# Cross-attention and the experts' shared part put into one block: the last two tiles' norm, logits and rank stand between the first pieces of the shared expert

## The chip, the cores and the metric

One NeuronCore of one Trainium2 chip. The metric is device time in microseconds (us) of the whole program, one launch, fp32 in and out; lower is better. The kernel before takes 1863.8 us (median of 3 runs).

## What is computed

One decoder layer without a norm at its end, on 4096 tokens (64 sequences of 64) of width 256:

```python
x = x + attn(layernorm(x))                     # 32 heads of 64, 8 KV heads, RoPE, causal, sinks
x = x + xattn(layernorm(x), ctx, ctx)          # 8 heads; softmax over (256 x 256) per head
h = layernorm(x)
logits = h @ router_w.T                        # 8 experts, top 1, score = sigmoid(top logit)
routed = sum_e down_e(up_e(xr_e) * silu(gate_e(xr_e)))    # xr_e = score * h for the expert's tokens
shared = (silu(h @ gate_w) * (h @ up_w)) @ down_w         # 256 -> 512 -> 256, for all tokens
x = x + shared + routed
```

## The kernel before, in words

Three blocks stand one after the other; between two blocks all engines wait for each other. Each engine (TensorE PE, ScalarE ACT, VectorE DVE, GpSimd POOL, and SyncE SP, which issues most DMAs) has a stream of its own, written out by hand; semaphores join them. Nothing reorders a stream: an instruction that waits holds up all behind it on its engine.

- `attention`: 32 tiles of 128 tokens. It leaves the stacked operands of the second attention in DRAM.
- `cross`: 32 tiles. A tile t goes through five stages, each in the body of a later tile: scores and row maxima (t), turned scores and exponentials (t+1), the sums over the values (t+2, `nd`), division by the denominators and the residual `x2` (t+3), then norm, transposed norm `xn3T`, logits, argmax, rank within the expert, and the scatter of the scaled row into its expert's list (t+4). The denominators go through DRAM: `nd` to `xden` by DMA, reciprocal on DVE (`invert`), out to `inv_d` and back, broadcast, as `xrden` (`inverses_out`, `inverses_in`), then `quotient` on POOL. So after tile 31's scores four more bodies follow (t = 32 to 35), the last two of which (t = 34 and 35) hold only the division, norm and routing of tiles 30 and 31. POOL also splits the shared expert's weights here into a high and a low part (`wshh`, `wshl`).
- `experts`: first the shared expert in 64 pieces n (16 groups g of 256 tokens, 4 columns of the 512 wide hidden layer each). PE does in piece n `up_s(n, 0)` (gate) and `up_s(n, 1)` (up), 6 matmuls of 256 columns each, then `down_s(n-1)`, 6 more. Between them stand ACT `gate_s` (Silu) and `high_h` (copy), DVE `hidden_s` and `low_h`. Per group, SP loads `xs` (`load_x`, 256 KB from `xn3T_d`) and the residual `xb` (`load_base`), and stores `base_d` (`store`); ACT `high_x` and POOL `low_x` split `xs`. Meanwhile DVE makes the table of the routed tiles (`count_tiles` to `pad_rows`), SP sends it through DRAM (`tab_d`, `tabr`), POOL writes 8 padding scatters, and ACT issues the loads of the experts' weights, 1.5 MB each, at pieces 2, 6, ... 30. Then the routed tiles: 40 of 128 rows, through `wexp`.

In `experts` SP's order for group g, and PE's for the pieces, are:

```python
for g in range(1, NG + 1):
    if 2 <= g + 1 < NG:
        load_x(g + 1)
    store(g - 1)
    if 2 <= g + 1 < NG:
        load_base(g + 1)
    if g == 4:  # tab_d out, wait for it, tabr in
```

Of the kernel before, what the change touches and what calls it, by code (L numbers as in the profile page):

```python
# [8 lines left out]
F32 = mybir.dt.float32  # L9
# [773 lines left out]
def cross(nc, A, G, NT, NRT):  # L783
# [6 lines left out]
    with ExitStack() as pb:  # L790
# [3 lines left out]
        def bank(name, n=1):  # L794
            return pb.enter_context(nc.psum_tensor(name, [P, n, 512], F32))

        bS = bank("bankX", 4)
        bT = bank("bankXT", 2)
        bN = bank("bankN")
        bM = bank("bankM")  # L800

# [9 lines left out]
        wraw = sb("wraw", [P, WE])  # L811
# [35 lines left out]
        G.s_scat = s_scat  # L847
# [8 lines left out]
            sem(n) for n in ("s_f3p", "s_f3", "s_lg", "s_top", "s_esc", "s_oh1", "s_rank", "s_pos", "g_sc", "c_fin", "s_xr3"))  # L856

# [19 lines left out]
        def tiles(eng, body):  # L877
# [12 lines left out]
        block = pb.enter_context(nc.Block())  # L890

        @block.sync
        def _(sp):
# [25 lines left out]

            def body(tile, one, two, three, four, five):  # L920
# [13 lines left out]
                if five:  # L934
                    yp = y[1] % 2
                    sp.wait_ge(s_x2, at(y) + 1)
                    sp.dma_start(G.x2_d[bass.ds(at(y) * P, P), :], x2[yp][:]).then_inc(s_fst[yp], 16)
# [16 lines left out]
                if five:  # L954
                    if not three:
                        sp.wait_ge(s_f3, at(y) + 1)
                    sp.dma_start(G.xn3T_d[:, :, bass.ds(at(y) * P, P)].rearrange("k p n -> p k n"), xn3T[:]).then_inc(s_fst[y[1] % 2], 16)
# [5 lines left out]
            tiles(sp, body)  # L963
            for p in range(2):
                sp.wait_ge(s_fst[p], 32 * (NT // 2))

        @block.gpsimd
        def _(pool):
# [96 lines left out]
            tiles(pool, body)  # L1065

        @block.scalar
        def _(act):
# [20 lines left out]

            def scale_row(y):  # L1090
# [14 lines left out]
            def body(tile, one, two, three, four, five):  # L1105
                w, v, z, y = prev(tile, 1), prev(tile, 2), prev(tile, 3), prev(tile, 4)
                for r in range(STEPS):
# [4 lines left out]
                    if five and r == 3:  # L1112
                        act.wait_ge(s_f3p, at(y) + 1)
                        o = prev(y, 1)
                        need(act, s_fst[o[1] % 2], (pair(o) + 1) * 32)
                        nc.scalar.activation(xn3T[:], bM[:, 0, 0:D].rearrange("p (k n) -> p k n", k=2),
                                             ACT.Copy).then_inc(s_f3, 1)
                    if five and r == 5:
                        act.wait_ge(s_top, at(y) + 1)
                        nc.scalar.activation(score[:, 0:1], top8[:, 0:1], ACT.Exp, scale=-1.0).then_inc(c_fin, 1)  # L1120
# [11 lines left out]
            tiles(act, body)  # L1132

        @block.vector
        def _(dve):
# [81 lines left out]
            tiles(dve, body)  # L1217

        @block.tensor
        def _(pe):  # L1220
# [108 lines left out]
            tiles(pe, body)  # L1329


def experts(nc, A, G, NT, NRT):
# [8 lines left out]
    with ExitStack() as pc:  # L1341
# [6 lines left out]
        def bank(name, n=1):  # L1348
            return pc.enter_context(nc.psum_tensor(name, [P, n, 512], F32))

        bk = [bank(f"bankG{i}") for i in range(2)]
        bS = bank("bankU", 2)
        b4 = bank("bankH")
        bX = bank("bankY", 2)
        b7 = bank("bankI")

        wexp = sb("wexp", [P, E * WE])
        cnt, ntile, cum, ones8, ge, lim, v0, bad, ptmp2 = (
            sb(n, [P, E]) for n in ("cnt", "ntile", "cum", "ones8", "ge", "lim", "v0", "bad", "ptmp2"))
        above = sb("above", [P, E, NT])  # L1360
        ei, si, dist = (sb(n, [P, 1]) for n in ("ei", "si", "dist"))
        tabf = sb("tabf", [P, 2])
        tabi = sb("tabi", [P, 2], I32)
        padx = [sb(f"padx{e}", [P, 1], I32) for e in range(E)]
        tabr = sb("tabr", [1, 2 * P], I32)
        xin = [sb(f"xin{p}", [P, D + 1]) for p in range(2)]
        xs = [sb(f"xs{p}", [P, 2, 2 * P]) for p in range(2)]
        xsl = [sb(f"xsl{p}", [P, 2, 2 * P], F32R) for p in range(2)]
        xsh = [sb(f"xsh{p}", [P, 2, 2 * P], F32R) for p in range(2)]
        hs = [sb(f"hs{p}", [P, 2 * P]) for p in range(2)]  # L1370
        hsl = [sb(f"hsl{p}", [P, 2 * P], F32R) for p in range(2)]
        hsh = [sb(f"hsh{p}", [P, 2 * P], F32R) for p in range(2)]
        xb = [sb(f"xb{p}", [P, 2, D]) for p in range(2)]
# [10 lines left out]
        s_xin, s_yst, s_x2in, s_gat, s_out = (  # L1384
            [sem(f"{n}{p}") for p in range(2)] for n in ("s_xin", "s_yst", "s_x2in", "s_gat", "s_scout"))
        s_xsh = sem("s_xsh")
        XIN = 16 * (NG // 2)
        s_tx, s_xT, s_g, s_u, s_silu, s_h, s_th, s_hT, s_d, s_y, s_tok = (
            sem(n) for n in ("s_tx", "s_xT", "s_g", "s_u", "s_silu", "s_h", "s_th", "s_hT", "s_d", "s_y", "s_tok"))
# [11 lines left out]
        block = pc.enter_context(nc.Block())  # L1401

        @block.sync
        def _(sp):
            def load_x(g):
                need(sp, s_xT, g - 1)
                sp.dma_start(xs[g % 2][:], G.xn3T_d[:, :, g * 2 * P:(g + 1) * 2 * P].rearrange(
                    "k p n -> p k n")).then_inc(s_xin[g % 2], 16)

            def load_base(g):  # L1410
                need(sp, s_yst[g % 2], 16 * (g // 2))
                sp.dma_start(xb[g % 2][:], x2_d[g * 2 * P:(g + 1) * 2 * P, :].rearrange(
                    "(i p) d -> p i d", i=2)).then_inc(s_x2in[g % 2], 16)

            def store(g):
                sp.wait_ge(s_y, 2 * (g + 1))
                sp.dma_start(base_d[g * 2 * P:(g + 1) * 2 * P, :].rearrange("(i p) d -> p i d", i=2),
                             xb[g % 2][:]).then_inc(s_yst[g % 2], 16)
# [10 lines left out]
            for g in range(2):  # L1429
                load_x(g)  # L1430
            for g in range(2):
                load_base(g)
            for g in range(1, NG + 1):
                if 2 <= g + 1 < NG:
                    load_x(g + 1)
# [3 lines left out]
                if g == 4:  # L1439
# [17 lines left out]
        def _(pool):  # L1457
            nc.gpsimd.memset(ones8[:], 1.0).then_inc(s_ones, 1)
            def low_x(g):
                pool.wait_ge(s_xsh, g + 1)  # L1460
                nc.gpsimd.tensor_tensor(xsl[g % 2][:], xs[g % 2][:], xsh[g % 2][:].bitcast(F32),
                                        ALU.subtract).then_inc(s_xT, 1)

            for g in range(5):
                low_x(g)
# [6 lines left out]
            for g in range(5, NG):  # L1472
                low_x(g)
# [43 lines left out]
        def _(act):  # L1517
            def high_x(g):
                act.wait_ge(s_xin[g % 2], 16 * (g // 2 + 1))
                need(act, s_u, NF * (g - 1))  # L1520
                nc.scalar.activation(xsh[g % 2][:], xs[g % 2][:], ACT.Copy).then_inc(s_xsh, 1)

            def gate_s(n):
                act.wait_ge(s_g, n + 1)
                need(act, s_d, n - 1)
                nc.scalar.activation(hs[n % 2][:], bk[n % 2][:, 0, 0:2 * P], ACT.Silu).then_inc(s_silu, 1)

            def high_h(n):
                act.wait_ge(s_h, n + 1)
                nc.scalar.activation(hsh[n % 2][:], hs[n % 2][:], ACT.Copy).then_inc(s_th, 1)  # L1530
# [14 lines left out]
            high_x(0)  # L1545
            high_x(1)
            for n in range(NS):
# [4 lines left out]
                if n % NF == 2 and n // NF < E:  # L1552
                    nc.scalar.dma_start(wexp[:, n // NF * WE:(n // NF + 1) * WE], A["wexp"][n // NF]).then_inc(s_w, 16)
# [3 lines left out]
        def _(dve):  # L1557
            ch = Chain(dve, c_tab, 17, 0)

            def count_tiles():  # L1560
                dve.wait_ge(s_ones, 1)
                ch(nc.vector.tensor_tensor(cnt[:], run[:], C["base"], ALU.subtract))
# [57 lines left out]
            def hidden_s(n):  # L1620
                dve.wait_ge(s_silu, n + 1)
                dve.wait_ge(s_u, n + 1)
                nc.vector.tensor_tensor(hs[n % 2][:], bS[:, n % 2, 0:2 * P], hs[n % 2][:], ALU.mult).then_inc(s_h, 1)

            def low_h(n):
                dve.wait_ge(s_th, n + 1)
                nc.vector.tensor_tensor(hsl[n % 2][:], hs[n % 2][:], hsh[n % 2][:].bitcast(F32),
# [16 lines left out]

            for n in range(NS):
                hidden_s(n)
                low_h(n)
                if n == 1:
                    count_tiles()
                if n == 2:  # L1650
                    sum_tiles()
                if n == 3:
                    expert_of()
                if n == 5:
                    row_of()
                if n == 6:
                    tile_table()
                if n == 7:
                    pad_limits()
                if n in (9, 10):  # L1660
                    pad_rows(n - 9)
# [7 lines left out]
        def _(pe):  # L1669
            pe.wait_ge(G.s_wshh, 6)  # L1670

# [84 lines left out]
            for n in range(NS):  # L1756
                up_s(n, 0, bk[n % 2][:, 0, 0:2 * P], s_g)
                up_s(n, 1, bS[:, n % 2, 0:2 * P], s_u)
                if n >= 1:
                    down_s(n - 1)  # L1760
            turn_in((0, 0))
# [47 lines left out]

def decoder(nc, A, NT, NRT):  # L1810
    assert NT * P == NTOK and NT % 4 == 0 and NT >= 24 and NRT % 2 == 0 and NRT + NT < P
    with ExitStack() as top:
        G = Shared(nc, top, NT, NRT)
        attention(nc, A, G, NT, NRT)
        with nc.sbuf_tensor("wshh", [P, WE], F32R) as wshh, nc.sbuf_tensor("wshl", [P, WE], F32R) as wshl:
            G.wshh, G.wshl = wshh, wshl
# [53 lines left out]
```

## Time and profile before

| | us |
|---|---|
| median of 3 runs (lowest, highest) | 1863.8 (1858.2, 1870.18) |
| profiled execution: time | 1864.66 |
| its span, first to last instruction | 1862.5 |
| PE busy | 1728.7 (93%) |
| DVE busy | 1185.5 (64%) |
| POOL busy | 840.6 (45%) |
| ACT busy | 813.0 (44%) |
| mean granted clock of PE | 0.974 |

Busy times are of one profiled execution. In the row of tenths, PE stands at 9 in nearly all of 40 slices of 46.6 us; the exceptions are the first, slice 31 (5), slices 32 to 34 (7), one 7 in the attention's end, and slices 35 and 38.

### The profile page before, as it was taken

Reading aid. Unit: us, or ns where it says so; the run is one execution under the profiler, and the core shown is the slowest. Engines: PE = TensorE matmul, PEld = TensorE weight load, DVE = VectorE, ACT = ScalarE, POOL = GpSimd, SP = SyncE. Lnnn points to the kernel's source line nnn. Section 1 sums busy time; section 2 is a strip of 40 time slices with the busy share of each in tenths; the row PEclk is TensorE's granted clock in tenths of the full one; section 3 lists DMA queues with packets and bytes.
Section 4 is the critical chain, followed back from the end, with each engine's and each line's share of the span. In section 5 each row is a group of like instructions: output and inputs, shape, how many; then the busy total and the mean of one; then the engine's idle time right before and its main releaser. Section 6 shows DMA issues by size and latency. Waiting matters only on the chain. (4 is left out here: it accounts for less than half of the span.)

```text
span 1862.5 us, 45291 instructions
## 1 busy us (share of the span) xinstructions
PE 1728.7 (93%) x15345; PEld 1390.9 (75%) x15441; DVE 1185.5 (64%) x2269; ACT 813.0 (44%) x1575; POOL 840.6 (45%) x1302
## 2 busy tenths in 40 slices
PE   3999999999999999999699999999995779999997
PEld 2888888888888888888577777777773779866664
DVE  5777777777777777777478888888882334422221
ACT  3334434433433444343247777777774324311111
POOL 4554655555555465555334444444444121144443
PEclk9999999999999999999879999999998799999999
DMA  5021111111112112111234444444442453222221
GB/s 183 19 58 44 42 56 54 36 51 56 42 42 56 47 37 56 56 39 42 75 101 111 123 119 117 115 118 124 123 109 63 167 207 125 74 64 67 66 64 39
DMA packets 145343, 148.43 MB, mean 80 GB/s; under 512 B 26194, under 2 KB 139926, under 8 KB 143482
## 3 DMA queue, kind: packets, MB, share of 16 engines
q1 hardware_dynamic: 138362, 120.87, 23.6%
q0 software_dynamic: 5760, 14.06, 2.4%
q10 hardware_dynamic: 1152, 12.58, 1.9%
q8 instruction: 43, 0.70, 0.2%
q14 instruction: 26, 0.21, 0.0%
HBM read 93.46 MB, written 54.11 MB: 79 GB/s over the span
## 5 line engine op out<-in xcount | busy, mean ns | idle before, releaser
L1149 DVE TENSOR_REDUCE xmax<-bankX 128x4 f32<-128x1024 f32 x256 | 309.2, 1218 | 63.4 <-PE bankX L1234 58.1
L1102 ACT ACTIVATE xe<-bankXT 128x512 f32<-128x512 f32 x512 | 292.1, 598 | 91.2 <-PE bankXT L1245 74.9
L1245 PE MATMUL bankXT<-stq,stk 98*128 98x256 f32 x1024 | 229.4, 310 | 11.4 <-ACT xe L1102 4.9
L369 POOL TENSOR_TENSOR roped<-ropeC,ropeD 128x512 f32<-128x512 f32 x160 | 205.4, 1290 | 56.4 <-DVE ropeD L530 56.3
L1245 PEld LDWEIGHTS bankXT<-stq,stk 98*128 98x128 f32 x1024 | 155.9, 191 | 54.1 <-ACT xe L1102 31.8
L557 DVE TENSOR_TENSOR oTl<-bankV,oTh 128x512 fp32r<-128x512 f32 x128 | 88.1, 688 | 166.7 <-ACT oTh L445 166.7
L662 PE MATMUL bankQ<-wqh,xnTh 128*128 128x512 f32 x384 | 188.9, 492 | 0.0
L1234 PE MATMUL bankX<-stk,stq 96*128 96x256 f32 x1024 | 172.6, 293 | 14.2 <-DMA rw<-in_rw 10.9
L361 POOL TENSOR_TENSOR prob<-prob,rden 128x1024 f32<-128x1024 f32 x64 | 122.0, 1906 | 88.6 <-DVE rden L553 88.6
L1234 PEld LDWEIGHTS bankX<-stk,stq 96*128 96x128 f32 x1024 | 146.2, 198 | 18.2 <-DMA rw<-in_rw 11.1
L728 PE MATMUL bankO<-woh,oTh 128*128 128x256 f32 x512 | 152.5, 298 | 0.0
L662 PE MATMUL bankQ<-wql,xnTh 128*128 128x512 f32 x384 | 152.2, 396 | 0.0
L662 PE MATMUL bankQ<-wqh,xnTl 128*128 128x512 f32 x384 | 151.9, 396 | 0.0
L713 PE MATMUL bankV<-probT,vbd 128*128 128x256 f32 x512 | 136.8, 390 | 9.8 <-ACT probT L439 9.8
L728 PE MATMUL bankO<-woh,oTl 128*128 128x256 f32 x512 | 143.3, 280 | 0.0
L728 PE MATMUL bankO<-wol,oTh 128*128 128x256 f32 x512 | 143.3, 280 | 0.0
L527 DVE TENSOR_TENSOR ropeC<-bankQ,const 128x512 f32<-128x512 f32 x160 | 109.5, 684 | 40.3 <-PE bankQ L662 40.3
L1260 PE MATMUL bankN<-xe,cT 128*32 128x256 f32 x2048 | 123.8, 382 | 0.4 <-ACT xe L1102 0.4
L439 ACT ACTIVATE probT<-bankP 128x512 f32<-128x512 f32 x128 | 76.2, 596 | 108.8 <-PE bankP L639 108.8
L445 ACT ACTIVATE oTh<-bankV 128x512 fp32r<-128x512 f32 x128 | 76.7, 599 | 103.5 <-PE bankV L713 103.5
L1007 POOL TENSOR_TENSOR xpart<-nd,xrden 128x512 f32<-128x512 f32 x32 | 41.1, 1286 | 173.3 <-DMA xrden<-inv_d 173.3
L329 POOL TENSOR_TENSOR spare_g<-half_neg 128x1 f32<-128x1 f32 x130 | 25.3, 195 | 203.9 <-DVE mv L499 199.3
(196 smaller groups left out, 4022.3 us busy)
## 6 DMA issues: line engine op xcount, KB each, us to landing
stackk_d<-chl SPq DMA_DIRECT2D x96, 128.0 KB, 2.3
stackq_d<-q2hl SPq DMA_DIRECT2D x96, 128.0 KB, 2.3
stk<-stackk_d SPq DMA_DIRECT2D x32, 384.0 KB
stq<-stackq_d SPq DMA_DIRECT2D x128, 96.0 KB
wexp<-in_wexp ACTq DMA_DIRECT2D x8, 1536.0 KB
x_d<-x SPq DMA_DIRECT2D x64, 128.0 KB, 1.9
xrden<-inv_d SPq DMA_DIRECT2D x64, 128.0 KB, 2.5
xin<-xg_d SPq DMA_DIRECT2D x40, 128.5 KB, 2.1
```

The lines of the kernel that those rows point to most:

```text
L361: nc.gpsimd.tensor_tensor(v, v, rden[:, r, :].unsqueeze(2).to_broadcast([P, 16, HD]), ALU.mult).then_inc(s_pn, 1)
L369: nc.gpsimd.tensor_tensor(roped[c % 3][:], ropeC[c % 2][:], ropeD[c % 2][:], ALU.add).then_inc(s_rsum, 1)
L527: nc.vector.tensor_tensor(ropeC[c % 2][:].rearrange("p (h d) -> p h d", d=HD), src.rearrange("p (h d) -> p h d", d=HD), cos.unsqueeze(1).t ...
L557: nc.vector.tensor_tensor(oTl[g % 2][:], bV[:, 0, :].rearrange("p (a b) -> p a b", a=4), oTh[g % 2][:].bitcast(F32), ALU.subtract).then_in ...
L662: ins = nc.tensor.matmul(out, a[p][:, k, :], w[:, k, col:col + 512], start=False, stop=(k == 1 and n == 2))
L713: ins = nc.tensor.matmul(out[:, :, b, :], vbd[u[1]][b][:, g, :], src[:, :, b, :], start=True, stop=True)
L728: ins = nc.tensor.matmul(out, a[g % 2][:, j, :], w[:, 4 * g + j, :], start=False, stop=(g == 3 and j == 3 and n == 2))
L1102: nc.scalar.activation(xe[q][:].rearrange("p n m -> p (n m)"), bT[:, q % 2, :], ACT.Exp).then_inc(s_xe, 1)
L1149: nc.vector.tensor_reduce(xmax[tile[1] % 2][:, :, a:b + 1:b - a].rearrange("p m h -> p h m"), bS[:, 2 * (pr % 2):2 * (pr % 2) + 2, :].rear ...
L1234: ins = nc.tensor.matmul(bS[:, q % 4, m * D:(m + 1) * D], stq[p][0:96, hd, m * P:(m + 1) * P], stk[p][0:96, hd // 4, :], start=True, stop= ...
L1245: ins = nc.tensor.matmul(bT[:, q % 2, n * D:(n + 1) * D], stk[p][0:98, hd // 4, n * P:(n + 1) * P], stq[p][0:98, hd, :], start=True, stop= ...
L1260: ins = nc.tensor.matmul(bN[32 * j:32 * j + 32, 0, (m % 2) * D:(m % 2 + 1) * D], c[:, k, 160 * j + 32 * m:160 * j + 32 * m + 32], xe[4 * b ...
```

## The change

`cross` and `experts` share one block, so that no engine waits for the others between them. The SBUF and PSUM that both use are now allocated together (`shared_memory`); `xs`, `xb` and `hs` lie in the buffer of the shared expert's raw weights, which is free once they are split. The bodies t = 34 and 35 of `cross` are gone; what they did for tiles 30 (`prior`) and 31 (`last`) is called between the first pieces of the shared expert, on each engine at a place of its own. The loads of `xs` for groups 0 and 1 are issued before the body t = 32, their split before t = 33. The experts' weights, whose buffer overlaps those of `cross`, are loaded at pieces 18, 23, ... 53. The table is made 12 pieces later and its DMA stands at g = 6; `load_x` runs two groups ahead in SP's order.

```diff
 # cross, tiles(): the last bodies
-            for t in range(LAST, NT + 4):
+            for t in range(LAST, NT + 2):
+                ahead_of(t)
                 peeled(t)
 # SP in cross
+            def ahead_of(t):
+                if t == NT:
+                    sp.wait_ge(G.s_wshh, 6)
+                    for g in range(2):
+                        load_x(g)
 # POOL, ACT in cross
+                if t == NT + 1:
+                    low_x(0)
+                if t == NT + 1:
+                    high_x(0)
 # SP in experts
-            for g in range(2):
-                load_x(g)
             for g in range(2):
                 load_base(g)
+            load_x(2)
+            inverses_out(last)
+            inverses_in(last)
+            store_x2(prior)
+            store_xn(prior)
             for g in range(1, NG + 1):
-                if 2 <= g + 1 < NG:
-                    load_x(g + 1)
+                if g + 2 < NG:
+                    load_x(g + 2)
                 store(g - 1)
                 if 2 <= g + 1 < NG:
                     load_base(g + 1)
-                if g == 4:
+                if g == 1:
+                    store_x2(last)
+                if g == 2:
+                    store_xn(last)
+                if g == 6:
                     sp.wait_ge(s_tabi, 1)
 # POOL in experts
+            low_x(1)
             nc.gpsimd.memset(ones8[:], 1.0).then_inc(s_ones, 1)
-            for g in range(5):
+            quotient(last)
+            weigh(prior)
+            low_x(2)
+            spread(last)
+            send(prior)
+            low_x(3)
+            weigh(last)
+            send(last)
+            for g in range(4, 8):
                 low_x(g)
             pool.wait_ge(s_pad, 1)
 # ACT in experts
-            high_x(0)
             high_x(1)
             for n in range(NS):
                 gate_s(n)
                 high_h(n)
                 if n % NF == 0 and 2 <= n // NF + 1 < NG:
                     high_x(n // NF + 1)
-                if n % NF == 2 and n // NF < E:
-                    nc.scalar.dma_start(wexp[...], A["wexp"][n // NF]).then_inc(s_w, 16)
+                if n == 2:
+                    evac_norm(prior)
+                if n == 4:
+                    exp_score(prior)
+                if n == 6:
+                    scale_row(prior)
+                # 9, 11, 13: the same for last
+                if n == 18:
+                    for q in range(2):
+                        act.wait_ge(G.s_scat[q], 16 * (NT // 2))
+                        act.wait_ge(G.s_fst[q], 32 * (NT // 2))
+                if n >= 18 and (n - 18) % 5 == 0 and (n - 18) // 5 < E:
+                    e = (n - 18) // 5
+                    nc.scalar.dma_start(wexp[:, e * WE:(e + 1) * WE], A["wexp"][e]).then_inc(s_w, 16)
 # DVE in experts, after hidden_s(n) and low_h(n)
+                # 0: invert(last); 1: normalise(prior); 3: choose(prior); 5: place(prior), stats_of(last)
+                # 7: normalise(last); 10: choose(last); 12: place(last)
-                # count_tiles to pad_rows at 1, 2, 3, 5, 6, 7, 9, 10
+                # count_tiles to pad_rows at 13, 14, 15, 17, 18, 19, 21, 22
 # PE in experts, after up_s(n, 0), up_s(n, 1), down_s(n - 1)
+                # 2: turn_norm(prior); 3: logits(prior); 4: rank(prior)
+                # 9: turn_norm(last); 10: logits(last); 11: rank(last)
```

(The comment lines for DVE, PE and the second tile of ACT stand for the same `if n == k:` form as the lines shown.)

## Rows read from the trace of the kernel before

**Rows 1.** Windows: us, busy us (instructions) by engine, granted clock, DMA share, GB/s.

```profile
1410.00:1420.00 10.00, 8.64 (x84) 5.53 (x88) 2.88 (x10) 6.96 (x16) 3.08 (x4) 1.00 0.29 83
1420.00:1430.00 10.00, 2.87 (x22) 1.86 (x14) 3.18 (x16) 1.69 (x4) 4.27 (x8) 0.75 0.21 62
```

**Rows 2.** Timeline, tile 31's chain and the seam: start, duration, engine, work, idle before.

```profile
1420.79 0.37 PE L1291 MATMUL bankM<-onehot,onesf 128*128 128x8 f32 x2
...
1422.85 0.51 ACT L1095 ACTIVATE xr<-xn,score 128x256 f32<-128x256 f32 x1 [1.57 <-POOL score L1030]
...
1423.79 0.35 DVE L1158 RECIPROCAL xiden<-xden 128x32 f32<-128x32 f32 x1 [1.02 <-DMA xden<-nd]
...
1430.56 1.26 POOL L1007 TENSOR_TENSOR xpart<-nd,xrden 128x512 f32<-128x512 f32 x1 [4.26 <-DMA xrden<-inv_d]
...
1444.33 1.11 POOL L1036 DMA_INDIRECT xg_d<-xr,posx  x1 [2.16 <-DVE posx L1197]
...
1448.98 0.91 SPq L1407 DMA_DIRECT2D xs<-xn3T_d  x2
...
1453.30 1.28 ACT L1526 ACT_TABLE_LOAD   x1
...
1454.04 0.55 PE L1688 MATMUL bankG<-xsh,wshh 128*128 128x256 f32 x1 [11.27 <-POOL xsl L1461]
...
1455.70 0.38 ACT L1526 ACTIVATE hs<-bankG 128x256 f32<-128x256 f32 x1 [1.11 <-PE bankG L1688]
...
1459.23 0.28 PE L1701 MATMUL bankY<-wshh,hsh 128*128 128x256 f32 x1
```

**Rows 3.** Timeline, one tile's norm, logits and rank on PE at full clock.

```profile
1416.33 0.38 PE L1224 MATMUL bankM<-const,xn 128*128 128x128 f32 x2
...
1417.77 0.55 PE L1285 MATMUL bankM<-rw,xn3T 128*128 128x8 f32 x4
```

**Rows 4.** Timeline, undisturbed pieces of the shared expert: ACT's group period, end.

```profile
1547.77 0.62 ACT L1521 ACTIVATE xsh<-xs 128x512 fp32r<-128x512 f32 x1
1556.41 0.62 ACT L1521 ACTIVATE xsh<-xs 128x512 fp32r<-128x512 f32 x1
...
1614.40 0.38 PE L1711 MATMUL bankI<-const,xin 128*128 128x128 f32 x2
```

**Rows 5.** Waits of PE, from 1454 us: us in total, times, longest.

```profile
PE bankY L1701 <- DVE hsl L1627: 15.0, 6, 6.6
```

**Rows 6.** Timeline, the four longest waits of PE, and the Silu before the last.

```profile
1481.47 0.38 PE L1701 MATMUL bankY<-wshh,hsh 128*128 128x256 f32 x1 [2.65 <-DVE hsl L1627]
...
1500.67 0.39 PE L1701 MATMUL bankY<-wshh,hsh 128*128 128x256 f32 x1 [2.34 <-DVE hsl L1627]
...
1519.67 0.58 PE L1701 MATMUL bankY<-wshh,hsh 128*128 128x256 f32 x1 [6.64 <-DVE hsl L1627]
...
1539.03 0.37 ACT L1526 ACTIVATE hs<-bankG 128x256 f32<-128x256 f32 x1
...
1540.82 0.40 PE L1701 MATMUL bankY<-wshh,hsh 128*128 128x256 f32 x1 [1.73 <-DVE hsl L1627]
```

**Rows 7.** Waits of ACT for loads of xs, from 1454 us.

```profile
ACT xsh L1521 <- DMA xs<-xn3T_d: 14.0, 3, 7.6
```

**Rows 8.** Timeline of SP's queue around the table at g = 4.

```profile
1505.44 0.47 SPq L1441 DMA_DIRECT2D tab_d<-tabi  x1
1513.76 0.26 SPq L1443 DMA_DIRECT2D tabr<-tab_d  x1
1514.07 0.39 SPq L1407 DMA_DIRECT2D xs<-xn3T_d  x1
```

**Rows 9.** Windows in the shared expert, columns as in Rows 1.

```profile
1500.00:1505.00 5.00, 3.28 (x25) 3.08 (x26) 2.37 (x7) 2.28 (x6) 1.83 (x2) 1.00 0.24 81
...
1520.00:1525.00 5.00, 5.00 (x28) 5.00 (x28) 0.95 (x3) 1.20 (x3) 0.00 (x0) 0.60 0.97 327
...
1555.00:1560.00 5.00, 5.00 (x44) 5.00 (x43) 2.41 (x7) 2.32 (x6) 1.30 (x1) 1.00 0.22 73
```

More of the change, by code:

```diff
@@ L875, in pair, with tiles @@
             return tile[0] * 2 + tile[1] // 2
-        def tiles(eng, body):
+        def tiles(eng, body, ahead_of):
             def peeled(t):
@@ L962, in _ @@
             sp.wait_ge(s_invz, 16)
-            tiles(sp, body)
-            for p in range(2):
-                sp.wait_ge(s_fst[p], 32 * (NT // 2))
+            tiles(sp, body, ahead_of)
         @block.gpsimd
@@ L1063, in body, with low_x, ahead_of @@
                     split_shared(at(tile) - 1)
-            tiles(pool, body)
+            def low_x(g):
+                pool.wait_ge(G.s_xs0, g + 1)
+                nc.gpsimd.tensor_tensor(G.xsl[g % 2][:], G.xs[g % 2], G.xsh[g % 2][:].bitcast(F32),
+                                        ALU.subtract).then_inc(G.s_xT, 1)
+            def ahead_of(t):
+                if t == NT + 1:
+                    low_x(0)
+            G.pool = quotient, weigh, send, spread, low_x
+            tiles(pool, body, ahead_of)
         @block.scalar
@@ L1112, in body @@
                     if five and r == 3:
[L1113 to L1117, printed above, removed]
+                        evac_norm(y)
                     if five and r == 5:
-                        act.wait_ge(s_top, at(y) + 1)
-                        nc.scalar.activation(score[:, 0:1], top8[:, 0:1], ACT.Exp, scale=-1.0).then_inc(c_fin, 1)
+                        exp_score(y)
                     if three and r == 6:
@@ L1130, in body, with high_x, ahead_of @@
                         exp_x(v, 2 * (r + STEPS - LAG) + 1)
-            tiles(act, body)
+            def high_x(g):
+                act.wait_ge(G.s_xin[g % 2], 16 * (g // 2 + 1))
+                need(act, G.s_u, FF // P * (g - 1))
+                nc.scalar.activation(G.xsh[g % 2][:], G.xs[g % 2], ACT.Copy).then_inc(G.s_xs0, 1)
+            def ahead_of(t):
+                if t == NT + 1:
+                    high_x(0)
+            G.act = evac_norm, exp_score, scale_row, high_x
+            tiles(act, body, ahead_of)
         @block.vector
@@ L1216, in _, with routing_of @@
             c_rt = sem("c_rt")
-            tiles(dve, body)
+            def routing_of(y):
+                return Chain(dve, c_rt, 4, at(y))
+            G.dve = invert, normalise, choose, place, stats_of, routing_of
+            tiles(dve, body, lambda t: None)
         @block.tensor
@@ L1327, in body @@
                         turn_ctx(w)
-            tiles(pe, body)
+            G.pe = turn_norm, logits, rank
+            tiles(pe, body, lambda t: None)
 def experts(nc, A, G, NT, NRT):
@@ L1470, in _ @@
                     in_=zeros[:], in_offset=None, bounds_check=DUMMY - 1, oob_is_err=False).then_inc(s_padd, 16)
-            for g in range(5, NG):
+            for g in range(8, NG):
                 low_x(g)
@@ L1517, in _ @@
         def _(act):
[L1518 to L1521, printed above, removed]
+            evac_norm, exp_score, scale_row, high_x = G.act
             def gate_s(n):
@@ L1669, in _ @@
         def _(pe):
+            turn_norm, logits, rank = G.pe
             pe.wait_ge(G.s_wshh, 6)
+            pe.wait_ge(G.s_xm, NT * 8)
             def three(a, b):
@@ L1760, in _ @@
                     down_s(n - 1)
+                if n == 2:
+                    turn_norm(prior, False)
+                if n == 3:
+                    logits(prior)
+                if n == 4:
+                    rank(prior)
+                if n == 9:
+                    turn_norm(last, False)
+                if n == 10:
+                    logits(last)
+                if n == 11:
+                    rank(last)
+            pe.wait_ge(G.s_pos, NT)
+            pe.wait_ge(G.s_nd, NT)
             turn_in((0, 0))
```

179 lines of the change are left out of this document (112 added, 67 removed).

## The prediction, as put on record before the changed kernel was run

> **What bounds the kernel now.** I read the share of busy time and the 40 slices first: PE is busy for 93% of the span and every other engine for 64% or less, so only places where PE stands still or runs at a lower clock are worth anything. Then the windows around the weak slices: PE runs at full clock up to 1420 us and then falls to 2.87 us busy in 10 [rows 1]. The timeline says what it waits for. Its last matmul of the second attention's steady work starts at 1420.79, the first one of the shared expert at 1454.04 [rows 2]. Between the two lies one chain through all engines: tile 31's denominators go out and back through DRAM, POOL divides, then norm, logits, rank and the scatter, issued at 1444.33; the blocks change, and SP issues the first load of `xs` at 1448.98, 3.5 us after the scatter's issue has ended; the load lands, ACT and POOL split it [rows 2]. Then I read the waits of PE in the shared expert: 15.0 us in six, all for `hsl` [rows 5]; the timeline dates the four longest (2.65, 2.34, 6.64, 1.73) [rows 6]. ACT's waits say whose they are: ACT waited three times, 14.0 us in all, for a load of `xs` [rows 7]; three of the four (2.65, 6.64, 1.73: 11.0 us) follow such a wait, the two at about 1500 (2.34 here and a 1.06 after it) do not. From 1617 us on the routed tiles keep PE full, and the chain of waits that ended last is PE's matmuls alone; the change doesn't touch them.
>
> A piece of the shared expert costs 18 matmuls. Undisturbed, ACT's split of `xs` comes at 1547.77 and at 1556.41 [rows 4]: 8.64 us for four pieces, 2.16 a piece, 0.12 a matmul. At half clock 28 matmuls take the 5 us in which 44 run otherwise [rows 9].
>
> **The seam: what goes.** PE has nothing to wait for at the end of body t = 33: groups 0 and 1 of `xs` need tiles 0 to 3 only, their loads are issued before SP's body t = 32, where SP waits for the reciprocal of tile 29 anyway, and POOL's split of group 0 stands ahead of a wait for `xrden` of more than 4 us (the like of the 4.26 in [rows 2]). I cost these at nothing. ACT's split of group 0 is 0.62 us [rows 4] in the ping-pong of turned scores and exponentials and delays PE's end of the attention from about 1421.3 to 1421.9; it disappears in the next wait, below.
>
> What is late next is ACT. Its row scaling for tile 29 ends at 1423.36 [rows 2]; it hangs on POOL, not on PE, so it stays. Behind it come the split of group 1 (0.62), the table load for Silu (1.28) and the first Silu, which so starts at 1425.3. From a Silu's start to the `down_s` that waits for its product I take 1.79 us (1539.03 to 1540.82) [rows 6]: `down_s(0)` starts at 1427.1. PE has finished the four `up_s` halves (24 matmuls, 2.9 us) at 1424.8 by then and stands still for about 2.3 us, which is in this sum. Before, `down_s(0)` started at 1459.23 [rows 2]. **This term is 1459.2 - 1427.1 = 32.1 us**, the 5 us of the first pieces at half clock included.
>
> **From `down_s(0)` to the last `down_s` but one.** Before: 1459.23 to 1614.40 [rows 2, 4], 155.2 us. Undisturbed it would be 62 x 2.16 + 0.72 = 134.6. The 20.6 between are waits of 14.4 (15.0 less 0.6 behind the end), about 5 at half clock after the waits for `xs` (in the 5 us of [rows 9] at 0.60, a 28 against 44 costs 1.8; the windows behind the other two gave 1.4 and 1.5), and 1.2 that I can't place.
>
> - The `xs` waits go. `load_x(g + 2)` is now issued where `load_x(g + 1)` was, or earlier, with one whole group (8.64 us) more until its use. It was issued some 4.8 us ahead of its use and took 3.0 us at the median, 7.6 at most; now it has over 13. At g = 6 the table's trip through DRAM stands ahead of `load_x(9)`: 8.3 us from `tab_d` to `tabr`, 0.3 to the load, 3.3 until it lands (ACT's wait for it ended at 1517.35) [rows 8]. Counted from ACT's split of group 7, `load_base` comes at +3.4, the load lands at +15.7, and the split of group 9 is due at +17.3: 1.6 us to spare, so a slow transfer could cost 1 to 5 us here. I take zero. Gain: 11.0 of waiting and 5 of clock.
> - The waits at about 1500 (3.4 us) stay: no load ends them; ACT came late there with "issue" and "remote" as releasers, while a weight transfer and POOL's padding scatters ran. Both still run, later. The 1.2 stays too. So does the rest: 134.6 + 3.4 + 1.2 = 139.2.
> - PE gets two tiles' norm, logits and rank, which lay in its idle time before: 0.38 + 0.55 [rows 3] and about 0.6 for the two rank products, 1.5 a tile, **+3.1**.
> - ACT gets two Exp between Silus. A load of tables was needed when the kernel first went from Exp to Silu, and none for the copies; if Exp is not in Silu's set, each of the two costs two loads, 2.56 us. At piece 4 ACT is free 2.4 us after the piece starts, then come 0.62 + 1.28 + 0.20 + 1.28, and 1.8 to `down_s`: 7.6. PE wants it after 2.16 + 0.6 (rank) + 2.16 + 1.44 = 6.4. **+1.2 to 1.3.** For tile 31 there is no split of `xs` in the same piece: **+0.6**.
> - DVE's placing and statistics stand between two pieces' products. No row shows this place; between nothing and the 1.3 of the Exp I take **0.7 for each tile**, since DVE is idle for over a third of a piece. The whole for both tiles: 1.9 + 1.4 = 3.3 us.
> - Clock: PE stands still for 2.3 us at the start. After the 2.34 at 1500 the granted clock stayed 1.00, after the 6.64 it was 0.60 for 5 us [rows 6, 9]. I take 1 us, between 0 and 3.
> - SP, POOL: SP issues three transfers (two `load_base`, `load_x(2)`), some 0.5 each, ahead of tile 31's inverses, and they are out before DVE's reciprocal of tile 31 (now behind `low_h(0)`, at 1427.1 instead of 1423.79) [rows 2]. The way from there to POOL's division took 6.4 us (1424.14 to 1430.56) [rows 2]: POOL divides at 1433.9 to 1436.9, waits for the Exp of tile 30, and splits group 2 until 1439.7; PE wants it at piece 8, about 1444. Some 4.5 us to spare: nothing. The later queue of POOL, with the wait for `weigh(last)` behind `low_x(3)`, has a piece or more to spare likewise. The weights: eight transfers 10.8 us apart instead of 8 to 15, the last at piece 53, 11 pieces or 23.8 us before the end; DMA was down to 73 GB/s 15 us after the last of them was issued at 1541 [rows 9]. Nothing.
>
> After: 139.2 + 3.1 + 3.3 + 1 = 146.6 against 155.2: **8.6 us gained.** Sum: 32.1 + 8.6 = 40.7. The profiled execution took 1864.66, so 1824.0; its time stands 0.9 above the median, so **1823 us**, 2.2% less.
>
> The table load is where a rule speaks against the change. The row shows 1.28 us; the load starts within 0.02 us of the end of the copy ahead of it, and the Silu at 1455.70 starts 1.12 after the load and just when PE delivers [rows 2]. The Trainium skill, "ScalarE: Activation LUTs", section "What ACT_TABLE_LOAD costs", gives 2.66 us for each switch, 1.28 of load and 1.38 of drain, and advises to batch by set. By it each Exp would hold Silu up for another 2.8 us, and the sum would be 1828 to 1829. The trace leaves room for at most 1.1 us behind the load, so this case's row disagrees with the whole figure.
>
> **Rivals.**
> 1. *Contention stays.* The waits for `xs` came from the weights' transfers filling the engines (327 GB/s in [rows 9]), and transfers queue up however early they are asked for; the table's trip at g = 6 hits a weight load as it did at g = 4. Then the 11 + 5 us stay: 1839. For it: each of the three waits lies in the stretch of the weights. Against it: the longest landing, 7.6, is well below the new 13. Chance 0.16.
> 2. *The last tiles hold up the pieces.* In order, every engine now serves both; if one link is late (xrden behind SP's transfers, `low_x(2)` behind the Exp), all pieces wait. The whole chain from reciprocal to rank was 19 us before; with 5 to 12 us of it uncovered: 1828 to 1836. For it: POOL has four waits in a row. Against it: the 4.5 us to spare. Chance 0.17.
> 3. *Slower, by the clock.* The two tiles' small matmuls and stalls break PE's stream, and it stays at 1.2 GHz over many pieces instead of falling for 5 us. A piece then costs 44/28 of 2.16, 3.4 us, 1.2 more; the 40.7 are used up after 34 of the 64 pieces, it is over 1% slower from 49 on, and at all 64 the time is 1901. For it: the clock fell to a mean of 0.75 within the 10 us in which PE went idle at the seam [rows 1]. Against it: between 1500 and 1505, with 3.28 of 5 busy, it stayed 1.00 [rows 9]. Chance 0.03.
> 4. *It doesn't do what it says*: the streams still wait for each other at the seam (the first split hangs on the last stores). Then only the later loads' gain is left, 1848. The first groups need tiles 0 to 3 only. Chance 0.02.
>
> **How the numbers follow.** The forecast (0.62): 1823, with the unknown costs between 1814 (no table loads, no placing, no kept stalls at 1500) and 1832. The range that leaves out no more than 2 in 10 takes in rival 2 and most of rival 1: 1813 to 1840. About 1%, 18.6 us, is what a measurement here tells from no change: faster 0.94, same 0.03, slower 0.03.
>
> **What would show it.** The first matmul of the shared expert at about 1422; `down_s(0)` at 1427; five table loads behind the attention's first one; ACT's waits for `xs` near zero and PE's waits in the shared expert at about 10 us in all instead of 15; the start of the routed tiles at about 1577 instead of 1617.6; the rest of the program as before. It is wrong if the shared expert still takes 155 us from `down_s(0)`, if its first matmul comes after 1430, or if the routed tiles wait for weights.

## The result, and the profile after

The changed kernel takes 1829.7 us (median of 4 runs, 1828.9 to 1830.8) against 1863.0 for the kernel before beside it; the ratio is 0.9823, 95% interval 0.980 to 0.9845. It is faster by 33 us or 1.8%; 1823 was forecast, in a range of 1813 to 1840. The profiled execution has a span of 1827.2 us, 35.3 less than before. One run of e1 below (2172 us, at a clock of 0.745) was far above the other three; medians and ratios here leave such runs out.

The two rows below are the page's 40 slices, of 45.7 us each. The list of slices in "Time and profile before" is partly miscounted: before, PE stands at 6 in slice 20, at 5, 7 and 7 in slices 31 to 33, at 7 in the last, and at 9 in slices 34, 35 and 38. After, only one 8 is left of the dent at the seam, in slice 32; the 8 and 6 in slices 20 and 21 are the start of the second attention.

```profile
PE   3999999999999999999869999999999899999997
PEclk9999999999999999999879999999999999999999
```

Windows of the changed kernel (us, busy us and instructions of PE, PEld, DVE, ACT, POOL, granted clock, DMA share, GB/s), to be read against [rows 1]:

```profile
1410.00:1420.00 10.00, 9.18 (x55) 5.42 (x56) 1.82 (x3) 5.90 (x14) 4.87 (x6) 0.66 0.23 70
1420.00:1430.00 10.00, 7.42 (x72) 6.20 (x72) 4.69 (x18) 5.42 (x12) 4.99 (x9) 0.94 0.41 121
1430.00:1440.00 10.00, 10.00 (x78) 10.00 (x77) 4.36 (x15) 4.17 (x9) 2.96 (x3) 0.89 0.28 81
```

PE is busy where it stood still before, but the granted clock in the stretch ahead of the seam is 0.66 on average, a mix of its two levels (1.2 and 2.4 GHz), and was 1.00. The timeline of the seam answers to [rows 2]:

```profile
1411.58 0.65 ACT L1171 ACTIVATE xsh<-wraw 128x512 fp32r<-128x512 f32 x1
...
1414.26 3.64 PE L1310 MATMUL bankN<-xe,cT 128*32 128x256 f32 x32
...
1423.17 0.37 PE L1341 MATMUL bankM<-onehot,onesf 128*128 128x8 f32 x2
1423.39 0.36 PE L1768 MATMUL bankX<-xsh,wshh 128*128 128x256 f32 x1
...
1424.59 1.28 ACT L1569 ACT_TABLE_LOAD   x1
...
1425.89 0.38 ACT L1569 ACTIVATE wraw<-bankX 128x256 f32<-128x256 f32 x1
...
1427.12 1.25 POOL L1087 TENSOR_TENSOR xsl<-wraw,xsh 128x512 fp32r<-128x512 f32 x1
1427.21 1.45 DVE L1689 TENSOR_TENSOR hsl<-wraw,hsh 128x256 fp32r<-128x256 f32 x1 [0.48 <-ACT hsh L1573]
...
1428.71 0.49 PE L1781 MATMUL bankXT<-wshh,hsh 128*128 128x256 f32 x1 [2.21 <-DVE hsl L1689]
```

The first matmul of the shared expert follows the attention's last by 0.2 us instead of 33. `down_s(0)` starts at 1428.71, 30.5 us earlier than in [rows 2]. (`xs`, `xb` and `hs` show as `wraw` now, the buffer they lie in.) The waits of PE from 1420 to 1585 us answer to [rows 5], those of ACT to [rows 7]:

```profile
PE bankXT L1781 <- DVE hsl L1689: 8.7, 6, 2.6
```

```profile
ACT xsh L1171 <- DMA wraw<-xn3T_d: 3.6, 1, 3.6
```

And the end of the shared expert, to be read against 1614.40 and 1617.59 before (the first is in [rows 4]):

```profile
1575.96 0.38 PE L1791 MATMUL bankM<-const,xin 128*128 128x128 f32 x2
...
1579.16 5.31 PE L1800 MATMUL bankX<-wexp,xT 128*128 x8 [1.26 <-DVE xT L1666]
1584.31 0.38 PE L1791 MATMUL bankM<-const,xin 128*128 128x128 f32 x2
```

From `down_s(0)` to the transpose of the first routed tile it takes 147.2 us, 7.9 less than before. 30.5 + 7.9 = 38.4 us are gained up to there, and 35.3 are left at the end: the first routed tile's 8 matmuls take 5.15 us here, and the same 8 took 3.54 before (half clock, 1.6 us). Of the last 1.5 us, 0.3 lie in PE's remaining 228 us, and 1.2 behind PE's last group of matmuls, which starts 12.9 us ahead of the end here and 11.7 before.

### The profile page after: what moved, and what is told of

The parts are those of the page before. It is cut to its first block and busy times, and to the rows that moved or that the text cites. A ratio compares the mean times of both kernels' runs of the same rounds, so it can differ in the third digit from the quotient of the medians.

```text
span 1827.2 us, 45302 instructions
## 1 busy us (share of the span) xinstructions
PE 1724.7 (94%) x15345; PEld 1385.0 (76%) x15441; DVE 1184.1 (65%) x2269; ACT 816.4 (45%) x1579; POOL 838.5 (46%) x1302
## 5 line engine op out<-in xcount | busy, mean ns | idle before, releaser
L1800 PE MATMUL bankX<-wexp,xT 128*128 x320 | 152.1, 599 | 2.3 <-DVE xT L1666 2.3
```

The source lines that it names most:

```text
L1800: ins = nc.tensor.matmul(out, xT[p][:, k, :], weights(base, (k * 2 + half) * FF, FF), start=(k == 0), stop=(k == 1))
```

## The experiments

Each ran on a chip beside the kernel before, whose medians were 1864.7 us beside e1 to e4, 1864.3 beside e5 to e8 and 1866.8 beside e9 to e11. "Waits" are the waits of PE for `hsl` in the shared expert unless another is named.

### Which part of the change brings what: e1 to e4

**e1** keeps the one block, the early loads and all other new places, but runs the bodies t = 34 and 35 whole ahead of the first piece.

```diff
-            for t in range(LAST, NT + 2):
+            for t in range(LAST, NT + 4):
-            # all calls for prior and last between the pieces, on every engine
```

> One block, the early loads of xs, the late weights and the new order of loads, but the bodies t = 34 and 35 stand whole ahead of the first piece, as before; nothing is called between the pieces. My theory (the overlap of the last two tiles' chain with the pieces carries most of the gain): the first down_s comes at about 1447 us instead of 1428.7, the stretch from it to the last but one takes 141 us instead of 147 (3.1 us of matmuls, 2.3 of waits behind the Exp and 1 of DVE work are gone), so 1842. Rival (the barrier and the loads behind it were the price, the overlap pays for itself only): 1830, as the changed kernel.

Measured: 1839.3 us (median of three runs, 1837.8 to 1844.3), ratio 0.987 (0.9837 to 0.9902). The first `down_s` comes at 1451.34 (PE's last matmul of body t = 33 was itself 1.9 us later than in the changed kernel), and the stretch from it takes 140.3 us. PE's waits for the norm of tiles 30 and 31 are back:

```profile
PE bankM L1276 <- DVE xn L1220: 12.4, 2, 8.2
PE bankXT L1740 <- DVE hsl L1663: 4.5, 2, 4.0
```

So the overlap is worth 9 us by the ratios and 10 by the medians, net of what it adds to the pieces, whose stretch is 6.9 us longer in the changed kernel's profile; one block, the loads' new places and the late weights bring the other 23 to 24. The price is rough: e1's interval is 6 us to either side, and its profiled run, the slowest of the three, lies 15 us above the changed kernel's.

**e2** and **e3** each put one edit alone into the kernel before.

```diff
# e2: SP
+            load_x(2)
             for g in range(1, NG + 1):
-                if 2 <= g + 1 < NG:
-                    load_x(g + 1)
+                if g + 2 < NG:
+                    load_x(g + 2)
# e3: ACT
-                if n % NF == 2 and n // NF < E:
+                if n >= 18 and (n - 18) % 5 == 0 and (n - 18) // 5 < E:
```

> The kernel before with one edit: load_x stands two groups ahead in SP's order, as in the change; weights and table stay where they were (pieces 2 to 30, g = 4). My theory (the place of load_x in the order ends the waits for xs): ACT's waits for xs fall from 14.0 us to under 3, PE's from 15.0 to about 4, time about 16 us less, 1848. Rival (the weights' transfers fill the engines, however early xs is asked for): waits stay, 1860 to 1866.

> The kernel before with one edit: the experts' weights are loaded at pieces 18, 23, ... 53, as in the change; load_x keeps its old place, the table its own. My theory: the waits for xs move with the weights and the table's trip at g = 4, now without a weight transfer beside it, gets shorter; two or three waits of 2 to 4 us stay: 1856 to 1862. Rival (it is the weights' place and pace that ends the waits): 1848.

Measured: e2 1852.7, ratio 0.994 (0.9926 to 0.9954); e3 1860.0, ratio 0.9983 (0.9968 to 0.9999). The waits of PE and of ACT in e2, from 1440 us (8.9 of ACT's 12.9 lie at the seam, before the first piece):

```profile
PE bankY L1702 <- DVE hsl L1628: 3.5, 2, 2.9
```

```profile
ACT xsh L1522 <- DMA xs<-xn3T_d: 12.9, 2, 8.9
```

In e3 the same two lines:

```profile
PE bankY L1702 <- DVE hsl L1628: 8.9, 6, 4.5
```

```profile
ACT xsh L1521 <- DMA xs<-xn3T_d: 22.8, 7, 9.1
```

The place in SP's order ends the waits, but for one: the 2.9 us in e2 stand behind the table's trip, where ACT waited 3.9 us for the load. The weights' place moves them: behind the seam ACT waits six times instead of three (the seventh, 9.1 us, is the seam's own). They cost PE less, 8.9 us instead of 15.0; 3.4 of the 6.1 less are the waits at about 1500, which have no load behind them and don't come in e3. e2's gain is 11 to 12 us where 16 were expected: the stretch from `down_s(0)` did shrink by 16 (139.3), but in that execution `down_s(0)` came 3.9 us later than before, and the first routed tile ran at half clock, as in the changed kernel. About 1 of the 3.9 stood there already at 1401 us. The rest came with the clock, which fell at the end of the attention as in the changed kernel, though ACT does no split there in e2: 32 small matmuls that took 1.93 us before took 3.64. In e3 the same 32 took 3.64 too, and `down_s(0)` came 3.3 us late, while the stretch from it shrank by 9.5 us (145.7), more than the 3 to 5 us that the whole program gained.

**e4** undoes the order alone in the changed kernel.

```diff
-            load_x(2)
             inverses_out(last)
-                if g + 2 < NG:
-                    load_x(g + 2)
+                if 2 <= g + 1 < NG:
+                    load_x(g + 1)
```

> The changed kernel with one part undone: load_x stands one group ahead in SP's order, as before. My theory: the waits for xs come back beside the weights and behind the table's trip, 8 to 12 us with the clock's share, 1838 to 1842. Rival (late weights alone do it): within 2 us of the changed kernel's 1829.7.

Measured: 1839.5, ratio 0.9869 (0.9843 to 0.9896), 9 to 10 us slower than the changed kernel.

```profile
PE bankXT L1780 <- DVE hsl L1688: 19.8, 9, 9.3
```

```profile
ACT xsh L1171 <- DMA wraw<-xn3T_d: 18.6, 5, 10.3
```

This settles rival 1: contention does not keep the waits once the loads are asked for a group earlier, save the one behind the table's trip.

### What is left in the changed kernel: e5 to e8

**e5** computes the score as 0.5 + 0.5 tanh(x/2).

```diff
-                nc.scalar.activation(score[:, 0:1], top8[:, 0:1], ACT.Exp, scale=-1.0)
+                nc.scalar.activation(score[:, 0:1], top8[:, 0:1], ACT.Tanh, scale=0.5)
-                nc.gpsimd.tensor_scalar(score[:, 1:2], score[:, 0:1], 1.0, None, ALU.add).then_inc(g_sc, 1)
-                pool.wait_ge(g_sc, at(y) + 1)
-                nc.gpsimd.tensor_tensor(score[:, 2:3], score[:, 1:2], minus[:], ALU.pow).then_inc(s_esc, 1)
+                nc.gpsimd.tensor_scalar(score[:, 2:3], score[:, 0:1], 0.5, 0.5, ALU.mult, ALU.add).then_inc(s_esc, 1)
```

> The changed kernel with the score computed as 0.5 + 0.5 tanh(x/2) instead of 1/(1 + exp(-x)); the same value, one POOL step less. If Tanh needs no other tables than Silu, the four loads between the pieces go. My theory (the loads hold up Silu, 1.4 and 0.9 us of PE's waits hang on them): those two waits go, 2.3 us, time 1827. Rival (DVE's placing would take their place, or the loads hide): within 1 us of 1829.7.

Measured: 1825.6, ratio 0.9792 (0.9779 to 0.9806), 4 us faster than the changed kernel. The changed kernel's timeline shows what goes, here for tile 30 at piece 4:

```profile
1439.12 1.28 ACT L1129 ACT_TABLE_LOAD   x1
1440.42 0.20 ACT L1129 ACTIVATE score<-top 128x1 f32<-128x1 f32 x1
1440.64 1.28 ACT L1569 ACT_TABLE_LOAD   x1
1441.93 0.38 ACT L1569 ACTIVATE wraw<-bankX 128x256 f32<-128x256 f32 x1
```

With Tanh the seam shows the first load for Silu and no other; the waits of 1.39 and 0.86 behind the two Exp are gone. One of 0.96 is left (1.11 in the changed kernel). It stands behind tile 31's placing, which the prediction had priced, but the placing doesn't make it: DVE's `low_h` does, which takes 2.05 us (1.96 in e5) instead of 0.43 while POOL issues tile 31's scatter and splits group 4. At its usual length it would have ended at 1465.66, ahead of the 1466.2 at which PE was ready for it.

```profile
1464.57 1.10 POOL L1056 DMA_INDIRECT xg_d<-xr,posx  x1 [5.43 <-ACT xr L1136]
1465.23 2.05 DVE L1689 TENSOR_TENSOR hsl<-wraw,hsh 128x256 fp32r<-128x256 f32 x1 [0.48 <-ACT hsh L1573]
...
1465.70 1.29 POOL L1087 TENSOR_TENSOR xsl<-wraw,xsh 128x512 fp32r<-128x512 f32 x1
...
1467.34 0.39 PE L1781 MATMUL bankXT<-wshh,hsh 128*128 128x256 f32 x1 [1.11 <-DVE hsl L1689]
```

All nine profiles with the last two tiles between the pieces have this, at 1.96 to 2.06 us. The other 2 us of the 4 I can't place; the intervals of the two ratios overlap, so they may be noise.

**e6** makes group 0's high part on POOL.

```diff
# POOL, ahead of body t = 33
+                    pool.wait_ge(G.s_xin[0], 16)
+                    nc.gpsimd.tensor_copy(G.xsh[0][:], G.xs[0]).then_inc(G.s_xs0, 1)
                     low_x(0)
# ACT, ahead of body t = 33
-                    high_x(0)
```

> The changed kernel with group 0's high part made on POOL, in its wait for xrden, instead of on ACT between the exponentials of body t = 33. My theory (ACT's 0.65 us there broke PE's stream, the clock fell to half for 4 us, and the last matmul of the attention came 2.8 us late, of which 1.4 reach the first down_s because the row scaling on ACT is next): the window 1410 to 1420 is back at clock 1.00, down_s(0) at about 1427.3, time 1828. Rival (the clock falls there for another reason): window and time as in the changed kernel.

Measured: 1829.5, ratio 0.9813 (0.980 to 0.9827): no gain in time that the measurement can show; the 1.4 us expected to reach `down_s(0)` are less than the interval's 2.6 us to either side. The steps came as expected, though. The window 1410 to 1420 has clock 1.00; from the rank product of tile 28 to that of tile 29 it takes 11.8 us instead of 14.6, from the former to `down_s(0)` 19.2 instead of 20.4. (`down_s(0)` itself is at 1429.97, not at 1427.3: this execution was 2.5 us later already at tile 28.) And PE waited 3.7 us at piece 28, where the changed kernel's profile has 2.6 behind the table's trip; e9 takes that up.

How firmly the split can be blamed for the clock, all 13 profiles tell. In eight of them the small matmuls of the tile before still take 1.93 us. Of these, the four with ACT's split (the changed kernel, e4, e5, e7) need 3.27 to 3.64 us for the 32 next ones, and the four without it (the kernel before, e6, e8, e9) 1.93. In the other five the clock has fallen a tile earlier for a reason that stays open; among them e2 and e3 need 3.64 us without any split. So the split brings the fall about, but isn't the only thing that does.

**e7** takes the table's trip apart.

```diff
                 if g == 6:
                     sp.wait_ge(s_tabi, 1)
                     sp.dma_start(tab_d, tabi[:]).then_inc(s_tabd, 16)
+                if g == 7:
                     sp.wait_ge(s_tabd, 16)
                     sp.dma_start(tabr[:], ...).then_inc(s_tab, 16)
```

> The changed kernel with the table's trip through DRAM taken apart in SP's order: tab_d goes out at g = 6, the wait for it and tabr stand at g = 7, behind load_x(9). My theory (the trip holds load_x(9) up: 3.6 us of ACT's wait, 2.6 of PE's, and half clock for some 4 us behind it): both go, ACT waits for no load of xs, time 4 us less, 1825.5. Rival (the weight transfer holds load_x(9) up wherever it stands): the wait stays, 1829.7.

Measured: 1829.3, ratio 0.9816 (0.980 to 0.9831): no gain. SP's queue shows that the load no longer waits (before, 7.9 us from `tab_d` to the load in the changed kernel):

```profile
1490.95 0.47 SPq L1481 DMA_DIRECT2D tab_d<-tabi  x1
1491.53 0.37 SPq L935 DMA_DIRECT2D wraw<-xn3T_d  x1
```

and ACT waits for no load. Yet PE waits 3.7 us at piece 28, and so it did in e5, e6 and e8. My theory was right about the wait for the load and wrong about the time: another wait stands there.

**e8** has the three edits, and gets two things out of the way to the first Silu.

```diff
# ACT, body t = 33, behind the last exponential
+                    if r == LAG and not inside(tile) and at(tile) == NT + 1:
+                        nc.scalar.activation(spare_a[:], G.half[:], ACT.Silu)
# ACT in experts
-            high_x(1)
             for n in range(NS):
                 gate_s(n)
                 high_h(n)
+                if n == 1:
+                    high_x(1)
```

> The changed kernel with the three edits together, and with Silu's tables loaded by a one column Silu in ACT's idle time in body t = 33 and the split of group 1 moved behind piece 1 on ACT (1.28 and 0.62 us out of the way to the first Silu). My theory: the terms add up, 2.3 + 1.4 + 4 + about 1.5, time 1820 to 1821; down_s(0) at about 1425.5. Rival (each removed wait uncovers the next): 1825 or more.

Measured: 1821.2, ratio 0.9766 (0.9752 to 0.978), the time expected, but not by the sum expected: that had 4 us for the table's trip, which e7 didn't give. From tile 28's rank product to `down_s(0)` it takes 4.9 us less than in the changed kernel. PE doesn't wait at the first `down_s` (1425.78) any more; the timeline shows the load in ACT's idle time and the first Silu 2 us earlier than in the changed kernel:

```profile
1420.23 1.28 ACT L1151 ACT_TABLE_LOAD   x1
...
1423.94 0.37 ACT L1569 ACTIVATE wraw<-bankX 128x256 f32<-128x256 f32 x1
...
1425.78 0.39 PE L1782 MATMUL bankXT<-wshh,hsh 128*128 128x256 f32 x1
```

### The wait that nobody released: e9 to e11

In e8 around piece 28, the three engines behind PE:

```profile
1489.98 0.39 ACT L1569 ACTIVATE wraw<-bankX 128x256 f32<-128x256 f32 x1 [2.65 <-PE bankX L1769]
...
1491.85 0.97 POOL L1514 DMA_INDIRECT xg_d<-zeros,padx  x1 [0.30 <-issue]
...
1492.87 0.42 DVE L1686 TENSOR_TENSOR wraw<-bankX,wraw 128x256 f32<-128x256 f32 x1 [5.09 <-remote]
```

DVE stands for 5.09 us with "remote" as releaser; the Silu that it needs had ended at 1490.37, 2.5 us before, and PE's matmuls earlier still. It goes on 0.05 us after the end of the last of POOL's eight padding scatters, which began at 1482.85. **e9** issues them one at a time, behind the splits of groups 6 to 14; **e10** keeps them in a row and moves the row to piece 44.

```diff
# e9
-            for g in range(4, 8):
+            for g in range(4, 7):
                 low_x(g)
             pool.wait_ge(s_pad, 1)
             for e in range(E):
                 nc.gpsimd.indirect_dma_start(...)      # cut: one padding scatter
+                if 7 + e < NG:
+                    low_x(7 + e)
-            for g in range(8, NG):
+            for g in range(15, NG):
                 low_x(g)
# e10
-            for g in range(4, 8):
+            for g in range(4, 12):
                 low_x(g)
             # cut: the eight scatters
-            for g in range(8, NG):
+            for g in range(12, NG):
                 low_x(g)
```

> The kernel of e8 with POOL's eight padding scatters one by one behind the splits of groups 6 to 14 instead of in a row at piece 24. In e5 to e8 ACT and DVE stood still for 3 to 5 us at piece 28 without waiting for a load or for an engine, while the scatters ran beside a transfer of weights; PE waited 3.7 us there. Theory P (the row of scatters holds the others up): no such wait anywhere, 3.7 us and some 2 us of half clock less, 1815 to 1817. Theory W (the transfer of weights alone does it, or the fetch of that stretch of code): the wait stays at piece 28, 1821.

> The kernel of e8 with the eight scatters in one row, but behind the split of group 11 (piece 44). Theory P: the wait moves to about piece 44 to 48 and keeps its size, 1821. Theory W: it stays at piece 28. If it is gone from both places, scatters, weights and the code of that stretch must meet: 1816.

> The changed kernel once more, for its profile. The wait behind the table's trip (2.6 us of PE), the clock in the window 1410 to 1420 and the 1.6 us of half clock in the first routed tile are of one execution. My theory: the Exp's waits (1.4, 0.9, 1.1 us) and the 2.2 at the first down_s come back with the same sizes, since order makes them; the clock's falls and the wait at pieces 28 to 32 may come elsewhere or be larger. Time 1829 to 1831.

Measured: e9 **1815.0** us (1814.8 to 1820.7), ratio 0.9741 (0.9719 to 0.9764); e10 1821.9, ratio 0.9775 (0.9751 to 0.9799); e11, the changed kernel once more, 1830.1, ratio 0.9813 (0.9789 to 0.9836). e9 and e10 ran beside the same runs of the kernel before; four of e9's five runs lie within 0.9 us, the fifth at 1820.7. In e9 the waits in the shared expert are nearly gone, and the stretch from `down_s(0)` takes 139.5 us instead of e8's 144.2:

```profile
PE bankXT L1783 <- DVE hsl L1691: 2.4, 4, 1.0
```

In e10 the wait has moved with the scatters, to 1529.65 (they ran from 1518.2 to 1528.1), and a smaller one stands where a load of `xs` was late by 2.2 us:

```profile
1510.57 0.39 PE L1782 MATMUL bankXT<-wshh,hsh 128*128 128x256 f32 x1 [1.20 <-DVE hsl L1690]
1529.65 0.39 PE L1782 MATMUL bankXT<-wshh,hsh 128*128 128x256 f32 x1 [3.33 <-DVE hsl L1690]
```

So theory P holds against W: the wait goes with the row of scatters, not with the stretch of code or the weights' transfers, which have the same places in e8, e9 and e10. e11's profile has the waits behind the Exp and the long `low_h` with the sizes of the first one to 0.01 us (1.39, 0.87, 1.12) and 3.67 at the scatters, and none behind the table's trip. The row is not enough by itself: in the first profile after, in e1 and in e2 it ran beside weights too, in e3 ahead of the first of them, and none of the four shows such a wait. (In e4 the engines soon waited for a load, and nothing can be told.) In the seven profiles that have it, DVE's standstill begins 4.9 to 5.7 us after the row does and ends within 0.15 us of the end of a scatter, the last one in six of them. What else must meet the row, and how scatters on POOL keep DVE and ACT from going on, stays open.

## Why the prediction was right, point by point

The direction, the order of the causes and the range were right; the gain was 33 us where 41 was the forecast. Between the profiles it is 35.3 against 40.7: 1.6 us are missing at the seam, 0.7 up to the routed tiles, 1.6 in the first of these and 1.5 behind it.

- **What bounds.** Right: the chain of tile 31 and the change of blocks for 33 us, then the waits for `xs`. e1 and e4 price both: 9 to 10 us for the overlap, and as much for the order of the loads.
- **The seam, 32.1 us.** 30.5, of which 0.4 stood there already at 1400 us. Two parts of the term were mis-sized. I let the 0.65 us of ACT's split "disappear in the next wait". It broke PE's stream instead, and the clock was at half for about 4 us (e6 and the count behind it): the 32 small matmuls took 3.64 us instead of 1.93, and PE's last rank product came at 1423.2 instead of 1420.8. The nd copy and the row scaling on ACT then hung on PE, which I had excluded ("it hangs on POOL, not on PE, so it stays"); 1.3 us reached `down_s(0)`, as e6 shows. And from Silu to `down_s` it took 2.8 us instead of 1.79, because DVE's `low_h(0)` took 1.45 us beside POOL's `low_x(1)`, and 0.43 for the next piece.
- **The waits for `xs`, 11 + 5 us.** Right by e2 (15.8 less in that stretch). In the changed kernel the spare time of 1.6 us at g = 6 was not enough in one of two profiles (3.6 us of ACT's wait, 2.6 of PE's; I had said 1 to 5 us for a slow transfer and taken zero).
- **"The waits at about 1500 (3.4 us) stay; both still run, later."** In the first profile after they are not there, in e11's they are, 3.7 us. The step failed in taking a wait that comes in some executions for a fixed one. Its suspects were the scatters and the weights' transfer; e9 and e10 point to the scatters.
- **Exp 1.2 and 0.6; placing 0.7 each.** The waits behind the Exp are 1.39 and 0.86 us, a good forecast. The placing cost nothing for either tile. The 1.11 us behind tile 31's are the price of POOL's scatter and split beside `low_h`, a term that the sum did not have; that 3.4 were measured where 3.3 were forecast is luck in this part. No run takes the 3.1 us of PE's own work on the two tiles apart.
- **Clock, 1 us of 0 to 3.** Too low. In the stretch from `down_s(0)`, 147.2 - 134.6 - 3.1 - 5.9 (waits) leaves 3.6 us, which the windows place at 1430 to 1440 and behind the 2.6 us wait. Two further falls, in body t = 33 and in the first routed tile (1.6 us), I had not in the sum at all.
- **SP, POOL, the weights: nothing.** Right for the queues: `quotient(last)`, `low_x(2)` and the weights held nobody up. Wrong for POOL's work beside DVE's: it lengthened `low_h` from 0.43 to 1.45 us at the seam and to 2.05 later. Rival 2 fell, rivals 3 and 4 too.

The sum from `down_s(0)` came out at 147.2 where 146.6 was forecast, partly because errors cancel: 3.4 kept and not there, 2.6 not expected and there, 1.2 unplaced and 2.6 more of the clock.

On the table loads the measurement decides against the page named in the prediction ("ScalarE: Activation LUTs", "What ACT_TABLE_LOAD costs", of the Trainium skill): in the excerpt under e5, the activation behind each load starts 1.30 and 1.29 us after the load does. A switch costs 1.3 us here, not 2.66.

## What to carry to other kernels

When two stages are joined so that the drain of one lies under the start of the next, walk each engine's list for what stands at the join: here a 0.65 us copy stood between exponentials, and a second copy and a table load on the way to the first Silu; moving all three gave 4.9 us up to `down_s(0)` (e8), more than the 3.1 us reckoned for PE's work on the two tiles. A load of a double buffer belongs in the queue as far ahead as the buffer allows; moved one group ahead, it took away most of the waits that looked like contention. A long row of small indirect scatters was better spread out: against one row at either of two places it gave 6 to 7 us (e9 against e8 and e10). All edits of e9 together give 1815 us, 0.8% below the changed kernel and 2.6% below the one before.

## What the runs showed of the hardware

- A standstill that no engine or load releases: beside eight padding scatters of about 1 us in a row on POOL, DVE stood for 3.7 to 5.1 us in the kernel before and in e5 to e8, e10 and e11 (5.09 to 5.12 in five of these), not in e1 to e3 nor in the changed kernel's first profile; with one scatter at a time (e9) it did not come.
- The granted clock fell to a mean of 0.66 (window 1410 to 1420) while PE ran short matmuls and never stood still for more than 0.5 us. In e6, with ACT's split out of that stretch, it stayed 1.00. e11's 0.67 in the same window doesn't bear on this, since its clock had fallen a tile earlier.
- DVE's subtraction with both operands in SBUF took 1.45 us when it started 0.09 us after a 1.25 us subtraction on POOL, and ended 0.29 behind it; 2.05 us beside a scatter's issue and a 1.29 us subtraction on POOL, ending 0.29 behind that too; 0.43 undisturbed. The Trainium skill ("SBUF — State Buffer", "SBUF: two separate sides") says of the port pair that the two share: "the other fully blocks". The row agrees.
- Tanh ran in the set of Exp and in that of Silu: no load stands between either and it (e5, e8).
